# Self-attention scores from two float32r parts, with two heads in two halves of the TensorE array

## The chip, the cores and the metric

One core of one Trainium2 chip (trn2) runs the whole program. The metric is the device time of one execution in microseconds (us). The engines have these names in the rows: PE is TensorE (PEld its weight loads), DVE is VectorE, ACT is ScalarE, POOL is GpSimd, and SPq is the queue of SyncE, which issues nearly all DMAs here.

## The reference, cut to what matters

Two batches of 1024 tokens with 256 features pass through a layer of cross-attention, self-attention and a GELU network, then routed experts, a second cross-attention with a prefix, and a ternary network. The change touches the self-attention of the first layer, 16 heads of 16 features in each batch, so 32 heads of 1024 queries and 1024 keys:

```
q, k, v = split_heads(x @ sq_w + sq_b), ...(sk), ...(sv)
scores = einsum('bqhd,bkhd->bhqk', q, k) / sqrt(16)
probs  = softmax(scores, axis=-1)
out    = einsum('bhqk,bkhd->bqhd', probs, v)
```

and the ternary weights of the last network, `clip(round(w / mean|w|), -1, 1)`, which are made beside the self-attention.

## The kernel before, in words

The program has a setup, a part "a" (cross-attention, and the projections of the self-attention, for each batch in turn), a stage "b0", the loop "b" over the 32 heads, a short part "w" (the ternary weights are transposed) and a long part "c" (all the rest). In "a" and "c" the order of the steps is written out by hand (`ORDER_A`, `ORDER_C`): every engine walks the same list and does its share of each step. In "a", step QK makes queries and keys of 512 tokens: PE multiplies (`self_qk`, L929), ACT takes each result out of PSUM twice (L1267 as a bf16 piece, L1268 as float32), DVE makes a second and a third bf16 piece from the rest (`pieces`, L1511, three operations L1516 to L1518), and SP stores the pieces in DRAM (`store_pieces`, L627). Step SV makes values (DVE L1524).

Scores need more than bf16. So a head's operands QX and KX lie in 96 rows (`QROWS`): three query pieces times three, two or one key pieces. `load_head` (L639) fetches them from DRAM with six DMAs. In `KX` three more rows hold ones, and in `QX` three rows hold minus the maximum of each query, in three bf16 pieces.

For a head the work comes in this order:

- `max_scores` (PE L950): 128 queries x 1024 keys in two matmuls; DVE takes the maximum (L1545). Two pairs of PSUM banks take turns, TR and the upper half of SCR.
- `split` on POOL (L1897) splits the maxima in three bf16 pieces, `maxima_transpose` on PE (L962) turns them, `maxima_rows` on DVE (L1557) copies them to `MT`, and `move_maxima` on SP (L653) writes them as three rows into QX with three DMAs.
- `t_scores` (PE L992): 128 keys x 1024 queries over 99 rows, two matmuls into two PSUM banks; ACT takes the exponential (L1283). Each matmul waits for the exponential before the last one, which frees its bank.
- `values` (PE L1003): probabilities times values and ones, four column groups of 32; the result is copied by ACT (L1276), turned by PE (L788), divided by DVE (L1563, L1566) and stored by SP (L651).

PE's program in a head: for each of eight key tiles `t_scores(kt)`, `values(kt - 1)` (the last tile's values come after the first scores of the next head) and `max_scores` of the head two later. The loop is unrolled by four heads, and at the fourth head the values are finished before the next group begins. The last two heads have no `max_scores`. The maxima of head n + 1 are turned at kt = 2 and copied by DVE at kt = 3 of head n. Between its maxima DVE also makes the signs of the ternary weights (L1591, L1594), and POOL multiplies them by the scale (L1922).

"b0" comes before the loop: after part "a" SP waits for all stored pieces, loads heads 0 to 2, then the ternary weights and two more weights (L665 to L668). PE and DVE make the maxima of heads 0 and 1. ACT meanwhile sums the absolute ternary weights (L1296, L1298). The first rows of maxima are moved, and the loop starts with PE's L992.

Of the kernel before, what the change touches and what calls it, by code (L numbers as in the profile page):

```python
# [30 lines left out]
DH = D // H  # L31
# [22 lines left out]
QROWS = 6 * DH  # L54
NS = 2 * TB + E - 1
UNROLL = 4
# [176 lines left out]
class Signal:  # L233

    TRIPS = {"setup": 1, "a": B, "b0": 1, "b": NH // UNROLL - 1, "blast": 1, "w": 1, "c": 1}

# [76 lines left out]
def build(nc, A, out):  # L315
    ctx = ExitStack()
    with ctx:
# [22 lines left out]
        PC = shared[:, o:o + 3072].bitcast(BF16).rearrange("p (e c n) -> p e c n", e=4, c=3)  # L340
        PTB = shared[:, o:o + 2048].rearrange("p (r n) -> p r n", r=2)
        o += 3072
        KB0 = shared[:, o:o + B * CHUNK_HEADS * SC].rearrange("p (b n) -> p b n", b=B)
        QX = [shared[:, o + 512 * j:o + 512 * (j + 1)].bitcast(BF16) for j in range(UNROLL)]
        KX = [shared[:, o + 2048 + 512 * j:o + 2048 + 512 * (j + 1)].bitcast(BF16) for j in range(UNROLL)]
        assert o + 4096 <= 3 * 4096
# [53 lines left out]
        HM = sb("HM", [128, 4, N])  # L400
        pscale = sb("pscale", [128, D])
# [12 lines left out]
        GB = MW[:, 4:8, :].rearrange("p (r j) d -> p r j d", r=2)  # L414
        tri = over("tri", [128, 128], BF16, "mask0")
# [35 lines left out]
        MT = sb("MT", [24, 128], BF16)  # L451
# [28 lines left out]
        scratch = nc.dram_tensor("pieces", [2, 3, NH * DH, S], BF16)  # L480
# [14 lines left out]
        def count(group):  # L495
# [33 lines left out]
        sq_full = Signal(sem("max_scores_full"), b0=2 * QT_PER_HEAD, b=UNROLL * QT_PER_HEAD,  # L529
                         blast=(UNROLL - 2) * QT_PER_HEAD)  # L530
        sq_done = Signal(sem("maxima_ready"), **sq_full.per)
        aux_full = Signal(sem("transposes_full"), 1, b0=1, b=2 * UNROLL, blast=2 * UNROLL - 1)
        aux_done = Signal(sem("transposes_taken"), 1, **aux_full.per)
        st_full = Signal(sem("t_scores_full"), 1, b=UNROLL * 16, blast=UNROLL * 16)
        st_done = Signal(sem("t_probs_ready"), 1, **st_full.per)
        pv_full = Signal(sem("head_out_full"), 1, b=UNROLL, blast=UNROLL)
        pv_done = Signal(sem("head_out_done"), 1, **pv_full.per)
        vh_ready = Signal(sem("head_values_ready"), b0=2, b=UNROLL, blast=UNROLL - 2)
        m_split = Signal(sem("maxima_split"), b0=2, b=UNROLL, blast=UNROLL - 2)
# [6 lines left out]
        signs_ready = Signal(sem("weight_signs_ready"), b=1 + KD, blast=1 + KD)  # L546
        tern_ready = Signal(sem("ternary_ready"), b=1, blast=1)
        mask1_ready = Signal(sem("mask1_ready"), setup=1)
        setup_done = Signal(sem("setup_done"), setup=1)
        d_head = [sem(f"head_loaded_{j}") for j in range(UNROLL)]  # L550
# [11 lines left out]
        def aux_value(tl, j, last, output):  # L562

            n = 0
            for jj in range(j + 1):
                n += not (last and jj == UNROLL - 1)
                if jj < j or output:
                    n += jj >= 1
            return Tally(tl.part, tl.i).next(aux_done, n)
# [5 lines left out]
        def _(sp):  # L575
            with nc.allow_non_contiguous_dma(reason="biases and small transposed loads"):
# [41 lines left out]

                for b in range(B):  # L620
# [6 lines left out]
                    def store_pieces(k):  # L627
                        for e in range(2 * KD):
                            sp.wait_ge(pc_ready.sem, tl.next(pc_ready))
                            dst = scratch[e // 2, :, :, :].rearrange("c r s -> r c s")[  # L630
                                bass.ds(b * D + (e % 2) * 128, 128), :, k * N:(k + 1) * N]
                            sp.dma_start(dst, PC[:, e]).then_inc(d_pieces, 16)

                    tl.walk(order_a, groups, {"PN": store_x1, "QK": store_pieces})
# [4 lines left out]
                def load_head(n, j):  # L639

                    src = scratch[:, :, bass.ds(n * DH, DH), :]
                    for c, r, m in ((0, 0, 3), (1, 3, 2), (2, 5, 1)):
                        rows = slice(r * DH, (r + m) * DH)
                        sp.dma_start(QX[j][rows, :], src[0, c].unsqueeze(0).to_broadcast([m, DH, S]))\
# [1375 lines left out]
```

## Time and profile before

| what | value |
|---|---|
| median of 3 runs | 1222.73 us (1219.84 to 1222.77) |
| profiled execution, its own time | 1223.43 us |
| its span | 1221.7 us |
| granted TensorE clock, mean | 0.944 |
| busy: PE, DVE, ACT, POOL | 90%, 68%, 50%, 23% |

The span is what the profile covers; 1.7 us lie around it. PE is busy most of the time, but busy includes waits inside the pipeline, so starts of matmuls say more than their durations. A line of a timeline gives the start, the length from the first start to the last end, engine, line of the kernel, output and inputs, and how many instructions are merged. A float32 matmul appears as two instructions.

### The profile page before, as it was taken

What the parts mean: (1) busy time and instruction counts of PE and PEld (TensorE: products, weight loads), DVE (VectorE), ACT (ScalarE), POOL (GpSimd) and SP (SyncE); (2) the same over time, 40 slices, a digit from 0 to 9 for tenths busy, and PEclk for the clock granted to TensorE, in tenths of its full rate; (3) what the DMA queues carried; (4) which work ended last, traced back from release to release, by engine and by line L of the source; (5) the groups of instructions that cost most, each with busy time, mean ns of one, the idle gap of its engine ahead of it and who ended that gap; (6) DMA issues with size and microseconds to landing.
All of it is one profiled execution on the core that took longest, in us unless ns stands there. A gap on an engine that the chain in (4) does not pass through costs nothing.

```text
span 1221.7 us, 20881 instructions
## 1 busy us (share of the span) xinstructions
PE 1101.5 (90%) x7648; PEld 603.6 (49%) x7648; DVE 829.6 (68%) x1453; ACT 610.7 (50%) x1159; POOL 285.8 (23%) x651
## 2 busy tenths in 40 slices
PE   6699689858999999999999889894989999999998
PEld 3366356502333333333333445663678877667665
DVE  1568658777888888888887327645374576987665
ACT  2265256406676766767667522130223345656643
POOL 3211212000100101001001124327238554621010
PEclk7799889958999999999999988987999999999999
DMA  7302100261122121221211331001015431110000
GB/s 193 55 11 70 60 2 23 91 196 61 34 68 60 39 63 34 69 62 35 63 34 40 126 105 35 9 9 69 27 57 178 148 100 44 39 35 2 12 11 31
DMA packets 102851, 73.34 MB, mean 60 GB/s; under 512 B 50738, under 2 KB 93791, under 8 KB 102495
## 3 DMA queue, kind: packets, MB, share of 16 engines
q1 hardware_dynamic: 99679, 63.61, 17.8%
q0 software_dynamic: 3072, 8.39, 2.1%
q8 instruction: 63, 1.03, 0.4%
q14 instruction: 37, 0.30, 0.1%
HBM read 42.94 MB, written 28.84 MB: 59 GB/s over the span
## 4 chain that ended last, share of the span: by engine, by line
PE 74%; DVE 13%; ACT 4%; issue 3%; POOL 2%; DMA 2%; SPq 1%; DVEq 0%; ACTq 0%; POOLq 0%
PE OUT L782 14%; PE TR L782 14%; PE OUT L1003 12%; PE SCR L992 9%; PE TR L788 8%; PE SCR L950 5%; PE TR L950 5%; PE TR L892 2%; PE OUT L788 2%; PE SCR L876 2%; ACT PTS L1239 2%; DVE small L1430 2%; PE SCR L869 2%; DVE small L1545 1%; POOL dispatched L1977 1%
## 5 line engine op out<-in xcount | busy, mean ns | idle before, releaser
L1283 ACT ACTIVATE shared<-SCR 128x512 f32<-128x512 f32 x512 | 277.8, 594 | 113.7 <-PE SCR L992 112.7
L1545 DVE TENSOR_REDUCE small<-TR 128x1 f32<-128x1024 f32 x128 | 156.8, 1225 | 48.9 <-PE TR L950 46.4
L1545 DVE TENSOR_REDUCE small<-SCR 128x1 f32<-128x1024 f32 x128 | 156.6, 1223 | 22.0 <-PE SCR L950 18.4
L1003 PE MATMUL OUT<-shared,HM 128*32 128x256 f32 x2048 | 163.7, 391 | 0.4 <-ACT shared L1283 0.4
L992 PE MATMUL SCR<-shared 99*128 99x512 bf16 x512 | 157.0, 382 | 4.7 <-DMA shared<-MT 4.4
L1856 POOL TENSOR_SCALAR small<-small 128x1 f32<-128x1 f32 x112 | 28.2, 252 | 398.1 <-DVE small L1431 396.4
L782 PE MATMUL TR<-xT,fifo 128*128 128x512 f32 x224 | 113.1, 665 | 2.8 <-ACT xT L1219 2.8
L950 PE MATMUL TR<-shared 96*128 96x512 bf16 x256 | 81.1, 400 | 15.4 <-DMA shared<-pieces 13.6
L1901 POOL CAST small<-small 128x8 bf16<-128x8 f32 x32 | 7.4, 231 | 371.4 <-DVE small L1545 371.4
L1219 ACT ACTIVATE xT<-TR 128x256 f32<-128x256 f32 x96 | 35.6, 382 | 115.8 <-PE TR L788 115.2
L1003 PEld LDWEIGHTS OUT<-shared,HM 128*32 128x32 f32 x2048 | 40.3, 108 | 102.7 <-issue 98.8
L1239 ACT ACTIVATE PTS<-TR 96x512 f32<-96x512 f32 x128 | 70.8, 591 | 35.6 <-PE TR L788 34.5
L992 PEld LDWEIGHTS SCR<-shared 99*128 99x128 bf16 x512 | 49.7, 97 | 76.2 <-ACT shared L1283 16.1
L950 PE MATMUL SCR<-shared 96*128 96x512 bf16 x256 | 81.3, 401 | 0.6
L788 PE MATMUL TR<-identf,P 128*96 128x128 f32 x512 | 74.0, 285 | 7.6 <-ACT PTS L1239 6.0
L782 PEld LDWEIGHTS TR<-xT,fifo 128*128 128x128 f32 x224 | 47.0, 216 | 61.7 <-issue 52.7
L1474 DVE TENSOR_REDUCE small<-SCR 128x16 f32<-128x1232 f32 (+1 forms) x32 | 48.7, 1521 | 38.9 <-PE SCR L876 38.8
L1857 POOL TENSOR_TENSOR small<-small 128x1 f32<-128x1 f32 x112 | 67.5, 603 | 9.3
L788 PEld LDWEIGHTS TR<-identf,P 128*96 128x96 f32 x512 | 53.1, 129 | 26.9 <-ACT PTS L1239 15.6
L782 PE MATMUL OUT<-fifo,shared 128*128 128x256 f32 x256 | 59.4, 386 | 3.2 <-ACT shared L1326 1.6
L782 PE MATMUL TR<-xT,fcT 128*128 128x512 f32 x128 | 55.7, 593 | 0.0
L782 PEld LDWEIGHTS OUT<-fifo,shared 128*128 128x128 f32 x256 | 48.4, 193 | 12.1 <-ACT shared L1326 2.6
(236 smaller groups left out, 1816.4 us busy)
## 6 DMA issues: line engine op xcount, KB each, us to landing
pieces<-shared SPq DMA_DIRECT2D x16, 384.0 KB, 2.5
shared<-pieces SPq DMA_DIRECT2D x64, 96.0 KB
HM<-dispatched SPq DMA_DIRECT2D x46, 128.0 KB, 2.2
expert_out<-HM SPq DMA_DIRECT2D x46, 128.0 KB
dispatched<-HB SPq DMA_DIRECT2D x6, 768.0 KB, 3.7
shared<-pieces SPq DMA_DIRECT2D x64, 64.0 KB
shared<-in_L_ffn_w SPq DMA_DIRECT2D x4, 1024.0 KB, 10.7
X<-in_x SPq DMA_DIRECT2D x1, 2048.0 KB, 9.0
```

Source lines behind the costliest of these rows:

```text
L782: ins = nc.tensor.matmul(dst, l, r, start=(n == 0), stop=(n == len(pairs) - 1))
L788: ins = nc.tensor.transpose(dst[0:m, n * width:n * width + p], s, ident[0:p, 0:p])
L950: ins = nc.tensor.matmul(pair[:, hf, :], QX[j][0:QROWS, kt * 128:(kt + 1) * 128], KX[j][0:QROWS, hf * 512:(hf + 1) * 512], start=True, sto ...
L992: nc.tensor.matmul(SCR[:, bank, :], KX[j][0:QROWS + 3, kt * 128:(kt + 1) * 128], QX[j][0:QROWS + 3, hf * 512:(hf + 1) * 512], start=True, ...
L1003: ins = nc.tensor.matmul(PV[32 * g:32 * g + 32, 0:256], VH[:, j % 2, kt, :], PTB[:, kt % 2, g * 256:(g + 1) * 256], start=(kt == 0), stop= ...
L1219: nc.scalar.activation(dst[:, :, c:c + 128], bank[:, 0:256].rearrange("p (k n) -> p k n", k=KD), ACT.Copy)\
L1239: nc.scalar.activation(PTS[0:KP, 4 * g:4 * g + 4, :], bank[0:KP].rearrange("p (h n) -> p h n", h=4), ACT.Copy)\
L1283: nc.scalar.activation(PTB[:, kt % 2, hf * 512:(hf + 1) * 512], SCR[:, bank, :], ACT.Exp, scale=DH ** -0.5).then_inc(st_done.sem, 1)
L1474: chain(nc.vector.tensor_reduce(mx, v, AX, ALU.max))
L1545: nc.vector.tensor_reduce(nm[:, r, kt:kt + 1], pair.rearrange("p h n -> p (h n)"), AX, ALU.max, negate=True)\
L1856: chain(nc.gpsimd.tensor_scalar(ve[:, r:r + 1], mv[:, r, 1:2], EPS, None, ALU.add))
L1857: nc.gpsimd.tensor_tensor(rstd[:, r:r + 1], ve[:, r:r + 1], minus_half, ALU.pow)\
```

## The change

The scores are made from two float32r parts of each number in place of three bf16 pieces, so a head has 48 rows (query parts 1, 1, 2 against key parts 1, 2, 1) plus three for the maxima. Heads lie in one of two halves of the partitions: head n in rows 0 to 50 or 64 to 114, by n // 2 % 2, and each QX and KX buffer holds two heads. In the loop each `t_scores` matmul of head n is followed at once by a `max_scores` matmul of head n + 2, which lies in the other half; `values` follow. The loop is no longer unrolled by four, so nothing is drained at each fourth head. Heads 0 to 3 are loaded at the beginning of batch 1 of part "a". The rows of ones come from 12 DMAs in the setup in place of four DVE memsets. A head's load is four DMAs, of 4 KB rows. The maxima are turned at kt = 3 (PE) and copied by ACT in place of DVE, behind its exponentials of kt = 3; the first such copy stands behind ACT's sums of the ternary weights. The head's output is divided by DVE at kt = 6 in place of 5. All ternary work is on POOL: three or four operations per piece. `pieces` on DVE is one operation in place of three.

```diff
-QROWS = 6 * DH
+QROWS = 3 * DH
-UNROLL = 4
+SLOTS = 4
...
+        PC = [over(f"pieces_{e}", [128, 2, N], F32R, "shared", o + 1024 * e) for e in range(2 * KD - 1)]
+        QX, KX = ([over(f"{name}_{r}", [128, S], F32R, "shared", o + 1024 * (2 * r + c)) for r in range(2)]
+                  for c, name in enumerate(("head_q", "head_k")))
...
-        scratch = nc.dram_tensor("pieces", [2, 3, NH * DH, S], BF16)
+        scratch = nc.dram_tensor("pieces", [2, 2, NH * DH, S], F32)
...
+        def half(n):
+            return 64 * (n // 2 % 2)
...
+                def load_head(n):
+                    src = scratch[:, :, n * DH:(n + 1) * DH, :]
+                    q, k, g = QX[n % 2][:, :].bitcast(F32), KX[n % 2][:, :].bitcast(F32), half(n)
+                    sp.dma_start(q[g:g + 2 * DH, :], src[0, 0].unsqueeze(0).to_broadcast([2, DH, S])).then_inc(d_head[n % SLOTS], 16)
+                    sp.dma_start(k[g:g + 2 * DH, :], src[1]).then_inc(d_head[n % SLOTS], 16)
+                    sp.dma_start(q[g + 2 * DH:g + 3 * DH, :], src[0, 1]).then_inc(d_head[n % SLOTS], 16)
+                    sp.dma_start(k[g + 2 * DH:g + 3 * DH, :], src[1, 0]).then_inc(d_head[n % SLOTS], 16)
...
+                    if b > 0:
+                        sp.wait_ge(d_pieces, DC + 16 * 4 * BLOCKS)
+                        for n in range(SLOTS):
+                            load_head(n)
...
+            def max_scores(tl, n, kt, hf):
+                if hf == 0:
+                    tl.next(sq_full)
+                    pe.wait_ge(sq_done.sem, tl.back(sq_full, 2))
+                rows = slice(half(n), half(n) + QROWS)
+                ins = nc.tensor.matmul(SQ[kt % 2][:, hf, :], QX[n % 2][rows, kt * 128:(kt + 1) * 128],
+                                       KX[n % 2][rows, hf * 512:(hf + 1) * 512], start=True, stop=True)
...
+                for kt in range(QT_PER_HEAD):
+                    for hf in range(2):
+                        t_scores(tl, n, kt, hf)
+                        if n + 2 < NH:
+                            max_scores(tl, n + 2, kt, hf)
                     if kt > 0:
+                        values(tl, n, kt - 1, 2)
+                    elif n > 0:
+                        values(tl, n - 1, QT_PER_HEAD - 1, 2)
+                    if kt == 3 and n + 1 < NH:
+                        maxima_transpose(n + 1)
+                    if kt == 5 and n >= 1:
+                        head_out_transposes(n - 1)
...
+            def maxima_rows(n):
+                act.wait_ge(aux_full.sem, taken["max", n])
+                act.wait_ge(d_m2, n * 48)
+                nc.scalar.activation(MT[:, :], AUX.bitcast(BF16)[0:24, 0:128], ACT.Copy).then_inc(aux_done.sem, 1)
...
-                        chain(nc.vector.tensor_tensor(rest, RR[:, e % 2, :], PC[:, e, 0, :], ALU.subtract))
-                        chain(nc.vector.tensor_copy(PC[:, e, 1, :], rest))
-                        nc.vector.tensor_tensor(PC[:, e, 2, :], rest, PC[:, e, 1, :], ALU.subtract)\
+                        nc.vector.tensor_tensor(PC[e][:, 1, :], RR[:, e % 2, :], PC[e][:, 0, :].bitcast(F32), ALU.subtract)\
...
+            def ternary(tl, chain, w, m, scaled):
+                below = TN[:, 0:w.shape[-1]]
+                chain(nc.gpsimd.tensor_scalar(below, w, wscale[:, 2, m:m + 1], None, ALU.is_lt))
+                chain(nc.gpsimd.tensor_scalar(w, w, wscale[:, 1, m:m + 1], None, ALU.is_gt))
+                ins = nc.gpsimd.tensor_tensor(w, w, below, ALU.subtract)
```

## Rows read from the trace of the kernel before

**Rows 1.** Windows: stretches before b0, b0, the loop with and without maxima:
```profile
0.00:256.77 256.77, 198.74 (x1527) 126.79 (x1527) 155.55 (x304) 113.66 (x197) 48.67 (x165) 0.89 0.23 65
256.77:280.09 23.32, 16.53 (x33) 2.33 (x34) 19.54 (x21) 5.37 (x20) 2.07 (x10) 0.50 0.65 207
280.09:667.00 386.91, 383.18 (x2972) 122.99 (x2972) 320.89 (x373) 270.47 (x513) 37.62 (x154) 0.99 0.19 52
667.00:686.63 19.63, 19.00 (x162) 5.66 (x161) 2.20 (x8) 16.52 (x33) 0.93 (x5) 1.00 0.07 9
```
**Rows 2.** Timeline of one key tile, PE and ACT (start, length):
```profile
406.86 0.60 PE L950 MATMUL TR<-shared 96*128 96x512 bf16 x2
407.31 0.60 PE L992 MATMUL SCR<-shared 99*128 99x512 bf16 x2
407.72 1.08 ACT L1283 ACTIVATE shared<-SCR 128x512 f32<-128x512 f32 x2 [0.46 <-PE SCR L992]
407.83 0.64 PE L1003 MATMUL OUT<-shared,HM 128*32 128x256 f32 x8
408.40 0.60 PE L950 MATMUL SCR<-shared 96*128 96x512 bf16 x2
```
**Rows 3.** Groups of DVE in the loop (busy, mean ns, idle before):
```profile
L1545 DVE TENSOR_REDUCE small<-TR 128x1 f32<-128x1024 f32 x120 | 147.0, 1225 | 42.1 <-PE TR L950 39.6 <-POOL small L1904 2.2
L1566 DVE TENSOR_TENSOR HM<-OUT,small 128x128 f32<-128x128 f32 x29 | 8.4, 291 | 1.0
L1563 DVE RECIPROCAL small<-OUT 128x8 f32<-128x8 f32 x29 | 5.8, 200 | 1.0 <-DVE xT L1594 0.4
```
**Rows 4.** Timeline of the last two heads, PE and ACT:
```profile
674.27 0.61 PE L992 MATMUL SCR<-shared 99*128 99x512 bf16 x2
...
679.18 0.69 PE L992 MATMUL SCR<-shared 99*128 99x512 bf16 x2
...
682.33 2.19 ACT L1283 ACTIVATE shared<-SCR 128x512 f32<-128x512 f32 x4 [0.44 <-PE SCR L992]
...
686.63 0.38 ACT L1276 ACTIVATE OSB<-OUT 128x256 f32<-128x256 f32 x1 [0.76 <-PE OUT L1003]
```
**Rows 5.** Line L992: weight loads (min, median, max ns):
```profile
L992 PEld LDWEIGHTS SCR<-shared x512: 95/97/152, 280.1 to 684.6; 99*128 99x128 bf16 x171
```
**Rows 6.** Timeline of a stage with float32r operands, weight load and matmul:
```profile
1210.26 0.28 PE L782 MATMUL OUT<-projT,hidH 128*128 128x256 f32 x1
1210.38 0.28 PE L782 MATMUL OUT<-projT,hidL 128*128 128x256 f32 x1
1210.26 0.19 PEld L782 LDWEIGHTS OUT<-projT,hidL 128*128 128x128 f32 x1
```
**Rows 7.** Timeline of matmuls in four row groups, and what follows:
```profile
1001.22 0.87 PE L876 MATMUL SCR<-KBW,QT 32*128 32x174 f32 x16
1002.02 0.48 PE L782 MATMUL OUT<-shared,MW 128*128 x1
```
**Rows 8.** Timeline from the last QK step to the loop:
```profile
234.33 7.13 PE L782 MATMUL TR<-xT,fifo 128*128 128x512 f32 x16 [0.47 <-ACT xT L1219]
244.70 0.69 DVE L1518 TENSOR_TENSOR shared<-HM,shared 128x512 bf16<-128x512 f32 x1
245.43 0.88 DVE L1524 TENSOR_TENSOR shared<-OUT,rows_a 128x256 f32<-128x256 f32 x2
256.77 1.01 PE L950 MATMUL TR<-shared 96*128 96x512 bf16 x2 [13.57 <-DMA shared<-pieces]
259.86 4.08 SPq L666 DMA_DIRECT2D xT<-in_L_ffn_w_proj  x1
273.94 0.42 ACT L1296 ACTIVATE XN<-xT 128x256 f32<-128x256 f32 x1 [31.01 <-DMA xT<-in_L_ffn_w_proj]
276.93 2.08 SPq L658 DMA_DIRECT2D shared<-MT  x3
279.12 0.18 ACT L1298 ACTIVATION_READ_ACCUMULATOR PTS<-xT 128x1 f32 x1
280.09 1.04 PE L992 MATMUL SCR<-shared 99*128 99x512 bf16 x2 [4.36 <-DMA shared<-MT]
```
**Rows 9.** DMAs by issue: KB each, us to landing:
```profile
pieces<-shared SPq DMA_DIRECT2D x16, 384.0 KB, 2.5
```
**Rows 10.** POOL's scaling of a ternary piece, group in the loop:
```profile
L1922 POOL TENSOR_TENSOR xT<-xT,small 128x256 f32<-128x256 f32 x7 | 4.3, 614 | 0.0
```

More of the change, by code:

```diff
@@ L559, in row @@
             return ap.rearrange("(o n) -> o n", o=1).to_broadcast([parts, ap.shape[0]])
[L562 to L569, printed above, removed]
+        taken = {("max", 0): aux_done.base["b0"] + 1}
+        for n in range(NH):
+            if n + 1 < NH:
+                taken["max", n + 1] = aux_done.base["b0"] + len(taken) + 1
+            if n >= 1:
+                taken["out", n - 1] = aux_done.base["b0"] + len(taken) + 1
+        taken["out", NH - 1] = aux_done.base["b0"] + len(taken) + 1
+        assert taken["out", NH - 1] == aux_done.total
+        def half(n):
+            return 64 * (n // 2 % 2)
         block = ctx.enter_context(nc.Block())
@@ L683, in head @@
                         sp.dma_start(xs_dram[i % B].rearrange("(s p) d -> p s d", p=128)[:, lo:hi, :], zeros).then_inc(d_zero, 16)
[L684 to L695 removed]
+                store_output(NH - 1)
                 for r in range(2):
@@ new lines, in t_scores, with values @@
+            def t_scores(tl, n, kt, hf):
+                bank = tl.slot(st_full, 2)
+                tl.next(st_full)
+                pe.wait_ge(st_done.sem, tl.back(st_full, 2))
+                rows = slice(half(n), half(n) + QROWS + 3)
+                nc.tensor.matmul(SCR[:, bank, :], KX[n % 2][rows, kt * 128:(kt + 1) * 128],
+                                 QX[n % 2][rows, hf * 512:(hf + 1) * 512], start=True, stop=True)\
+                    .then_inc(st_full.sem, 1)
+            def values(tl, n, kt, ahead):
+                pe.wait_ge(st_done.sem, tl.back(st_full, ahead))
+                if kt == 0:
+                    pe.wait_ge(pv_done.sem, tl.value(pv_full))
+                    pe.wait_ge(vh_ready.sem, n + 1)
+                for g in range(4):
+                    ins = nc.tensor.matmul(PV[32 * g:32 * g + 32, 0:256], VH[:, n % 2, kt, :],
+                                           PTB[:, kt % 2, g * 256:(g + 1) * 256], start=(kt == 0),
+                                           stop=(kt == QT_PER_HEAD - 1))
+                if kt == QT_PER_HEAD - 1:
+                    ins.then_inc(pv_full.sem, 1)
+                    tl.next(pv_full)
```

367 lines of the change are left out of this document (122 added, 245 removed).

## The prediction

> **What bounds the kernel now.** I read the windows first. The loop over heads takes 386.9 us with maxima and 19.6 us for the two heads without [rows 1], 406.5 us from its first PE start to the last head's copy [rows 8, 4], a third of the time. PE is busy 99% of it at full clock (0.99, the 2.4 GHz level), DVE 83%, ACT 70%. The timeline of one key tile shows the order in which PE spends it [rows 2]: two maxima products start at 406.86, two score products at 407.31, the values at 407.83, the next maxima at 408.40. That is 0.45 + 0.52 + 0.57 = 1.54 us per tile, and eight tiles with some 0.3 us of transposes make 12.6 us a head; 32 heads give 403 us, near the 406.5. ACT sits idle 0.46 us in each tile and waits for L992, and DVE waits for L950 (42 us for half of its maxima, [rows 3]). So PE's sequence is the bound, and whatever it sheds counts until another loop closes.
>
> Ahead of the loop lie two waits on other things. After the last pieces (DVE, until 245.4) PE stands 13.57 us, until a head's load has landed at 256.77 [rows 8]. Then b0 runs at DVE's pace, at clock 0.50 (the 1.2 GHz level) [rows 1], and the loop's first product waits until 280.09 for the rows of maxima.
>
> **The change, part by part, against the profiled execution's 1223.4 us (0.7 above the median of the runs).**
>
> *Products in two halves.* Three terms: the cost of a float32r product, whether two of them run at once, and what then closes the loop. A stage with float32r operands starts a 256-column matmul every 0.12 us [rows 6], just over 256 columns at 2.4 GHz, so a 512-column one should take some 0.22 us, what the bf16 ones take now (two in 0.45). I take a pair of a score and a maxima product at 0.22 + 0.03 us. PE's need per tile falls from 1.54 to 0.50 + 0.09 + 0.57 = 1.16 us (0.09 is what L992 now takes over its two streams before the values begin).
>
> What closes the loop then? The last two heads show it, since they have no maxima: from 674.27 to 679.18 are four tiles, 1.23 us each [rows 4], and the two heads together take 19.6 us, 1.22 a tile [rows 1], though PE would need 1.1. There each second score product waits for the exponential that frees its bank, and the values and the next tile stand behind it. This chain remains. It grows by the weight load that such a wait exposes: 0.19 us for float32r against 0.10 for bf16 [rows 6, 5], so +0.09, and by the 0.03 of the maxima products between. I get 1.22 + 0.09 + 0.03 = 1.34 us per tile, 10.7 us a head. DVE alone needs eight maxima at about 1.19 (a duration of 1.225 with ends overlapped) and 0.55 us for the head's output with its waits [rows 3], 10.0 us. ACT needs 16 x 0.53 (four in 2.19 us, [rows 4]) + 0.39 + 0.2 for the maxima's copy, 9.1 us. Both fit below 10.7, but DVE closely: it is next in line. Bounds: 10.0 us (DVE alone) to 12.6 (no overlap, as now).
>
> Loop: 30 heads x 10.7 + 2 x 10.5 (9.8 now, plus 8 x 0.09) + 0.9 for start and end = 343 us, against 406.5: **-63.5 us**. The drain at each fourth head goes with it, and the ternary signs leave DVE; they lay beside PE's work and are worth nothing by themselves. POOL takes them: at most four operations of about 0.61 us [rows 10] in a head of 10.7 us, ahead of a split that waits for the head's last maxima anyway. If that cover went, the maxima's split would be late; it has more than three tiles of slack. On SP a head's load is four issues in place of six, so what stands behind it (the maxima's rows, the output's store) is not later than now.
>
> *Pieces and the end of part a.* The last QK step is paced by PE (7.13 us for its 16 instructions, until 241.5), but DVE's three operations, 1.92 us per product, end at 245.4 [rows 8]. With one operation of 0.69 the end is 241.5 + 1.3 (ACT) + 0.7 = 243.5, 1.9 us earlier. I give the last QK of batch 0 the same 1.9, and the two QKs in the middle of a batch 0.5 each, where other work hides DVE: **-2.9 us** ahead of the last step. Bounds 0 to -6.
>
> *Early head loads.* PE no longer waits for the load; it starts b0 when the last values are out of PSUM, at 243.5 + 0.9 = 244.4 in place of 256.8. But b0 does not end by DVE alone. The first rows of maxima now stand on ACT behind its sums, which wait for the ternary weights. Those are issued when the last pieces are stored, 243.5 + 2.5 [rows 9] = 246.1 in place of 259.4, so 13.3 us earlier. Sums started at 273.94 and ended at 279.3; they will start at 260.6 and end at 266.0. Copy 0.2 and the move as now (280.09 - 276.93 = 3.16) give 269.5. DVE's 16 maxima, 244.4 + 1.1 + 19 = 264.6, are earlier. So the loop starts 280.1 - 269.5 = **10.6 us** sooner; the ends are -16 (DVE decides) and -5 (the loads land later behind the larger stores). The 12 DMAs for the rows of ones and the 16 for heads 0 to 3 lie on SP beside work of the setup and of batch 1, where only stores of tokens stand behind them. Nothing waits for those within several us.
>
> Sum: 1223.4 - 63.5 - 2.9 - 10.6 = **1146 us**. Part w and part c (535 us) stay.
>
> A rule against this change: the Trainium skill (TensorE: Matmul & The Clock Gate, Part 3, "The mechanism") says that a weight load overlaps running matmuls only when its row group differs. Its consequence is a rival below.
>
> **The rivals.**
>
> *Late rows of maxima.* The rows are turned at kt = 3 now, after three tiles and a block, near 5.1 us into a head; ACT copies at about 5.9; SP's three issues and the landing take 3.16 [rows 8], so they are there at 9.1 of 10.7 us. The slack is 1.6 us, where it was about 3. For it: four heads' worth of 4 KB rows may stand before them on the rings. If the landing grew by 3 us, each head waits 1.4 to 1.5 us: 31 x 1.45 = 45 us, time 1191. Chance 0.13.
>
> *Exposed weight loads.* The second score product and the second maxima product use the row groups of the first ones. If their loads wait until the first stream is through, 0.19 us [rows 6] come on per tile, 1.5 a head: 32 x 1.52 = 49, time 1195. Against: float32r loads start every 0.12 us though each lasts 0.19, between matmuls of the same rows [rows 6]. This is what the page's rule would do here, and the row speaks against the rule. Chance 0.13.
>
> *Halves in sequence, loads hidden.* 4 x 0.216 + 0.09 + 0.57 = 1.53 per tile, 12.65 a head: 30 x 12.65 + 22 = 401, time 1223.4 - 5.1 - 13.5 = 1205. Against it stands L876. Chance 0.07.
>
> *Slower.* The halves run in sequence and each load is exposed too: 4 x (0.216 + 0.19) + 0.66 = 2.29 us per tile on PE, 18.7 a head, 583 us for the loop, time 1386. It ends slower than before once a tile costs over 1.61 us: (406.5 + 13.5 - 22) / 30 = 13.3 us a head, less 0.4 for transposes, over 8. For it: no row shows float32r in row groups. Against: each half of it is absent where it could show [rows 6, 7]. Chance 0.06, and I add 0.01 for a clock that falls to 1.2 GHz in the loop. The heads without maxima kept 1.00 with PE streaming about 70% of the tile [rows 1, 4].
>
> *It brings nothing, some wait of its own eating all.* Chance 0.02.
>
> **How the numbers follow.** The forecast has 0.58 and its own range is 1130 to 1168: 10.3 to 11.2 us a head (-12 to +16), and the front's ends (-8 to +6). I predict 1146. The range reaches to the two rivals of 0.13 each: 1130 to 1197, with about 0.8 in it. About 0.3% is what a measurement of this kernel can tell from no change. Faster: 0.58 + 0.13 + 0.13 + 0.07 = 0.91; same 0.02; slower 0.07.
>
> **What would show it.** Right: L950 and L992 starts within 0.05 us of each other, a head every 10.7 us, DVE idle under 1 us a head, PE's first L992 near 267. L992 waiting for ACT in nearly every tile, with a weight load of 0.19 ahead of it, confirms the chain. Late maxima would show as L992 waiting for the DMA from MT at each head. Exposed loads would show as a gap of 0.4 us between first and second score products that no exponential explains. In sequence: a score and a maxima product start 0.22 us apart. Part a should end 3 to 5 us earlier. The prediction is wrong if heads take over 12 us or under 10 us, or if the loop starts after 272.

## The result and the profile after

The changed kernel takes 1173.1 us (median of 4 runs, 1169.1 to 1174.8) against 1222.8 us before (median of 4): a ratio of 0.959, 95% interval 0.954 to 0.963. The profiled execution takes 1171.8 us, its span 1169.7. The forecast was 1146 us, range 1130 to 1197.

The windows of the changed kernel, with the columns of [rows 1] (busy time of PE, weight loads, DVE, ACT, POOL with counts in brackets, then granted clock, DMA share, GB/s), b0 first and then the loop:
```profile
242.48:265.95 23.47, 17.66 (x35) 7.50 (x35) 19.89 (x21) 5.66 (x21) 3.28 (x13) 0.57 0.56 200
266.00:286.00 20.00, 19.77 (x109) 6.79 (x109) 11.02 (x9) 10.77 (x21) 3.61 (x9) 0.50 0.00 1
...
290.00:295.00 5.00, 5.00 (x37) 1.70 (x35) 3.14 (x3) 3.37 (x7) 0.00 (x0) 0.66 0.09 34
295.00:300.00 5.00, 5.00 (x46) 2.00 (x48) 4.61 (x6) 3.98 (x9) 1.07 (x6) 1.00 0.56 168
300.00:560.00 260.00, 259.56 (x2322) 103.98 (x2320) 238.51 (x234) 212.11 (x423) 64.08 (x176) 1.00 0.23 59
```
DVE is now busy 92% of the stretch from 300 to 560 (238.5 of 260), where it had 83%, so the loop is denser, as meant. But the loop runs its first 27 us at clock 0.50, the 1.2 GHz level. (It was 1.00 when b0 began and fell to 0.50 inside b0, near 245.6.) In the kernel before, it rose at 284, 4 us after the loop's start:
```profile
280.09:284.00 3.91, 3.91 (x12) 1.25 (x16) 1.88 (x2) 1.79 (x4) 0.00 (x0) 0.50 0.21 61
284.00:288.00 4.00, 4.00 (x37) 1.23 (x29) 2.41 (x5) 2.67 (x6) 0.00 (x0) 1.00 0.10 38
```

The timeline from the last QK step to the loop, to be held against [rows 8]. L784 is the product, L1494 DVE's one operation on the pieces, L952 the maxima product, L963 the score product, L1266 ACT's sums, L1259 its copy of the maxima, L673 their move:
```profile
232.22 7.13 PE L784 MATMUL TR<-xT,fifo 128*128 128x512 f32 x16 [0.47 <-ACT xT L1196]
240.76 0.69 DVE L1494 TENSOR_TENSOR pieces<-RR,pieces 128x512 fp32r<-128x512 f32 x1 [1.02 <-ACT RR L1245]
242.48 0.70 PE L952 MATMUL TR<-head_k,head_q 48*128 48x512 f32 x2 [1.39 <-issue]
244.65 0.58 SPq L679 DMA_DIRECT2D xT<-in_L_ffn_w_proj  x1
252.44 0.42 ACT L1266 ACTIVATE XN<-xT 128x256 f32<-128x256 f32 x1 [11.78 <-DMA xT<-in_L_ffn_w_proj]
262.36 0.27 ACT L1259 ACTIVATE MT<-OUT 24x128 fp32r<-24x128 bf16 x1 [4.52 <-PE OUT L984]
262.65 2.07 SPq L673 DMA_DIRECT2D head_q<-MT  x3
265.95 0.76 PE L963 MATMUL SCR<-head_q,head_k 51*128 51x512 f32 x1 [3.62 <-issue]
```
PE's 13.6 us of waiting is 1.4, and the loop starts at 265.95 instead of 280.09. POOL had split the maxima of head 0 by 254.3, but their transpose (L984) stands in PE's order behind the maxima products of head 1, so it starts only at 262.04, 7.7 us later. No run moves it.

Two key tiles of the loop, PE alone (start, length, the idle time in brackets; a matmul's row includes the load that stands exposed ahead of it):
```profile
400.46 0.49 PE L963 MATMUL SCR<-head_q,head_k 51*128 51x512 f32 x1
400.46 0.49 PE L952 MATMUL TR<-head_k,head_q 48*128 48x512 f32 x1
400.79 0.41 PE L963 MATMUL SCR<-head_q,head_k 51*128 51x512 f32 x1
400.80 0.41 PE L952 MATMUL TR<-head_k,head_q 48*128 48x512 f32 x1
401.14 0.64 PE L974 MATMUL OUT<-shared,HM 128*32 128x256 f32 x8
401.71 0.50 PE L963 MATMUL SCR<-head_q,head_k 51*128 51x512 f32 x1
401.71 0.50 PE L952 MATMUL SCR<-head_k,head_q 48*128 48x512 f32 x1
402.12 0.18 PEld L963 LDWEIGHTS SCR<-head_q,head_k 51*128 51x128 f32 x1 [0.23 <-ACT shared L1279]
402.13 0.50 PE L963 MATMUL SCR<-head_q,head_k 51*128 51x512 f32 x1
402.56 0.64 PE L974 MATMUL OUT<-shared,HM 128*32 128x256 f32 x8
```
A score and a maxima product start within 0.01 us of each other, in both pairs of both tiles. The first tile takes 1.25 us, the second 1.45: there the second pair waits for ACT's exponential, and its load of 0.18 us stands in the open. Such tiles alternate, 1.345 us on average. The largest idle times of the weight loader ahead of the score products, from 300 to 560 (us in total, times, longest):
```profile
PEld SCR L963 <- ACT shared L1279: 81.5, 257, 0.4
PEld SCR L963 <- DMA head_q<-MT: 4.0, 8, 0.6
```
The 81.5 us aren't all loss: some of these times are 0.41 us, ahead of a tile's first load while the values still stream, and the others 0.23, as at 402.12. PE itself is busy 259.6 of the 260 us.

The last two head outputs are copied here; the one before them is copied at 610.48:
```profile
621.55 0.39 ACT L1253 ACTIVATE OSB<-OUT 128x256 f32<-128x256 f32 x1
632.02 0.38 ACT L1253 ACTIVATE OSB<-OUT 128x256 f32<-128x256 f32 x1 [0.76 <-PE OUT L974]
```

Of the 51.6 us between the two profiled executions, the loop's earlier start gives 14.1 (13.5 forecast) and the loop itself 40.4 (366.1 us against 406.5, from its first score product to the last output copy; 63.5 forecast). Parts w and c take 2.6 us more (537.7 against 535.1). The 23 us missing in the loop are what the experiments had to find.

My first reading gave them to two places: some 10 us to the low clock (the first head's output comes 19.0 us after the loop's start and the second 14.3 later, where most later ones come every 11.09), and 12 us to a head of 11.1 us instead of 10.7.

### The profile page after: what moved, and what is told of

It is laid out like the page before. It is cut to its first block, busy times and chain, and to the rows that moved or that the text cites. A ratio compares the mean times of both kernels' runs of the same rounds, so it can differ in the third digit from the quotient of the medians.

```text
span 1169.7 us, 20774 instructions
## 1 busy us (share of the span) xinstructions
PE 1067.8 (91%) x7648; PEld 625.3 (53%) x7648; DVE 792.1 (68%) x1337; ACT 615.2 (53%) x1191; POOL 331.6 (28%) x724
## 4 chain that ended last, share of the span: by engine, by line
PE 75%; DVE 11%; ACT 4%; issue 3%; POOL 3%; DMA 2%; SPq 1%; DVEq 0%; ACTq 0%; POOLq 0%
PE SCR L963 16%; PE TR L784 16%; PE OUT L784 14%; PE OUT L974 12%; PE TR L790 8%; PE TR L894 2%; PE OUT L790 2%; PE SCR L878 2%; ACT PTS L1216 2%; DVE small L1409 2%; PE SCR L871 1%; POOL dispatched L1899 1%; POOL small L1784 1%; DVE small L1517 1%; PE SCR L952 1%
## 5 line engine op out<-in xcount | busy, mean ns | idle before, releaser
L963 PE MATMUL SCR<-head_q,head_k 51*128 51x512 f32 x512 | 218.2, 484 | 4.3 <-issue 3.6
L974 PE MATMUL OUT<-shared,HM 128*32 128x256 f32 x2048 | 168.8, 402 | 0.2 <-ACT shared L1279 0.2
L963 PEld LDWEIGHTS SCR<-head_q,head_k 51*128 51x128 f32 x512 | 92.9, 189 | 137.1 <-ACT shared L1279 114.8
L952 PE MATMUL SCR<-head_k,head_q 48*128 48x512 f32 x256 | 122.3, 516 | 1.2 <-DVE small L1517 0.8
L784 PE MATMUL TR<-xT,fifo 128*128 128x512 f32 x224 | 113.1, 665 | 2.8 <-ACT xT L1196 2.8
L952 PE MATMUL TR<-head_k,head_q 48*128 48x512 f32 x256 | 100.3, 474 | 2.3 <-issue 1.4
L784 PEld LDWEIGHTS TR<-xT,fifo 128*128 128x128 f32 x224 | 46.9, 215 | 61.8 <-issue 52.8
L784 PE MATMUL OUT<-fifo,shared 128*128 128x256 f32 x256 | 59.3, 386 | 3.2 <-ACT shared L1305 1.6
L784 PE MATMUL TR<-xT,fcT 128*128 128x512 f32 x128 | 55.7, 593 | 0.0
L784 PEld LDWEIGHTS OUT<-fifo,shared 128*128 128x128 f32 x256 | 48.4, 193 | 12.1 <-ACT shared L1305 2.6
## 6 DMA issues: line engine op xcount, KB each, us to landing
shared<-in_L_ffn_w SPq DMA_DIRECT2D x4, 1024.0 KB, 10.7
```

The costliest lines, as they stand in the source:

```text
L784: ins = nc.tensor.matmul(dst, l, r, start=(n == 0), stop=(n == len(pairs) - 1))
L952: ins = nc.tensor.matmul(SQ[kt % 2][:, hf, :], QX[n % 2][rows, kt * 128:(kt + 1) * 128], KX[n % 2][rows, hf * 512:(hf + 1) * 512], start=T ...
L963: nc.tensor.matmul(SCR[:, bank, :], KX[n % 2][rows, kt * 128:(kt + 1) * 128], QX[n % 2][rows, hf * 512:(hf + 1) * 512], start=True, stop=T ...
L974: ins = nc.tensor.matmul(PV[32 * g:32 * g + 32, 0:256], VH[:, n % 2, kt, :], PTB[:, kt % 2, g * 256:(g + 1) * 256], start=(kt == 0), stop= ...
```

## The experiments

**1. The two products apart.** Only the order on PE changes: both score products, the values, then both maxima products.
```diff
                         t_scores(tl, n, kt, hf)
-                        if n + 2 < NH:
-                            max_scores(tl, n + 2, kt, hf)
...
                     if kt == 5 and n >= 1:
                         head_out_transposes(n - 1)
+                    if n + 2 < NH:
+                        for hf in range(2):
+                            max_scores(tl, n + 2, kt, hf)
```

> The changed kernel with one edit: in each key tile both score products, then the values, then both maxima products (the order of the kernel before), so no score product has a maxima product of the other half beside it; operands, rows and loads stay. If the two halves really run at once in the changed kernel, this takes it away: a head goes from 11.1 us to 12.6 to 12.9 us (two streams of 0.43 us and 0.09 us of switch come on per tile, less what the chain of exponentials leaves idle), time near 1220. Rival, that the halves bring nothing and the gain is only the lost drain at each fourth head and the early loads: a head stays at 11.1 us, time 1172. The clock at the start of the loop: if it stayed low because TensorE had gaps in its stream there, it rises within about 5 us of the loop's start here, as in the kernel before; if it stayed low because a product in half the rows counts for less, it stays at 1.2 GHz for over 20 us here too.

Measured: 1196.6 us (one run), a head every 12.24 us, the loop 395.6 us. That is less than the 12.6 to 12.9 us and 1220 us that I expected, but far from the rival's 11.1. Standing beside each other is worth 1.13 us a head, and 29.5 of the 40.4 us that the loop gained. Without it the loop is still 10.9 us shorter than before; the lost drain, the operands and DVE's lighter work changed together there, and no run splits them. The clock was at 0.50 here too, until about 283, 19 us after the loop's start:
```profile
266.00:282.00 16.00, 16.00 (x87) 5.79 (x87) 8.43 (x7) 8.22 (x16) 1.25 (x2) 0.50 0.00 1
282.00:284.00 2.00, 2.00 (x16) 0.65 (x12) 1.23 (x1) 1.40 (x3) 0.14 (x1) 0.65 0.00 0
```
PE was busy for all of those 16 us. So idle time that the profile would show isn't what kept the clock down.

**2. Products in all rows ahead of the loop.** Twelve matmuls of 512 columns over all 128 rows, whose result nobody reads, stand behind the first maxima transpose, where PE would wait for the rows of maxima.
```diff
             maxima_transpose(0)
+            for _ in range(12):
+                nc.tensor.matmul(OUT[:, 1, :].rearrange("p (a n) -> p a n", n=128), identb[:, :],
+                                 onesb[:, :].unsqueeze(1).to_broadcast([128, 4, 128]), start=True, stop=True)
```

> The changed kernel with 12 dense bf16 matmuls of 512 columns, on no one's data, put on TensorE behind the first transpose of maxima, where it waits 3.9 us for the rows of maxima. Theory: the loop lost about 10 us because TensorE's clock stayed at 1.2 GHz for its first 27 us; the dense work lifts the clock before the loop and the loop holds it, so the first two heads take 12.5 + 11.1 us in place of 19.0 + 14.3, less up to 1.3 us for matmuls that run past the wait: 1163 to 1166. Rival: the loop's start is slow for another reason (first loads, POOL's ternary work, DVE), or the clock falls again at once: 1172 to 1174.

Measured: 1156.8 us (median of 5 runs, 1156.0 to 1162.4), ratio 0.947, interval 0.944 to 0.950. Windows:
```profile
264.00:268.00 4.00, 3.96 (x12) 1.31 (x10) 0.00 (x0) 0.23 (x1) 3.50 (x7) 0.57 0.01 2
268.00:272.00 4.00, 3.58 (x29) 1.43 (x29) 3.67 (x3) 3.36 (x7) 0.38 (x1) 1.00 0.00 0
```
The clock is at 1.00 from 268 and stays there. The loop takes 355.9 us in place of 366.1, and every head 11.10 us, the second one too. So the low clock cost 10.2 us inside the loop. The spans differ by 9.4 us (1160.3 and 1169.7), as the loop starts 1.15 us later in this execution; the medians differ by 16.3, and the profiles explain only the 9.4. The profiled execution is the slowest of the five (1162.4 us; the others take 1156.0 to 1157.1). The median lies below my 1163 to 1166; the heads came as the theory said.

**3. The same twelve in 48 rows.** The number and the columns are as above, the rows as in b0.
```diff
-                nc.tensor.matmul(..., identb[:, :],
-                                 onesb[:, :].unsqueeze(1).to_broadcast([128, 4, 128]), start=True, stop=True)
+                nc.tensor.matmul(..., identb[0:48, :],
+                                 onesb[0:48, :].unsqueeze(1).to_broadcast([48, 4, 128]), start=True, stop=True)
```

> As the version with 12 products of 512 columns ahead of the loop, but they use 48 rows of the array instead of 128. If the granted clock follows how dense the stream is, the result is that of the full-row products: first output copy about 12.4 us after the loop's start, 1155 to 1160 us. If it follows how many rows are at work too, the clock stays at half speed as in the changed kernel: first output copy 18 to 19 us after the start, second head above 13 us, 1170 to 1176 us.

Measured: 1164.4 us (one run). The clock did not rise with them:
```profile
264.00:268.00 4.00, 3.74 (x13) 1.96 (x11) 0.87 (x1) 1.08 (x2) 3.07 (x4) 0.50 0.00 0
...
284.00:288.00 4.00, 4.00 (x32) 1.15 (x24) 2.72 (x3) 2.56 (x6) 0.30 (x1) 0.66 0.15 36
```
The first output copy comes 19.2 us after the loop's start, as the second theory has it. The second head (11.9 us) is faster than expected, as the clock rose near 286.7 and not near 293, and the time lies below that theory's 1170 to 1176 us. So with the same number of products and columns the clock was up at the loop's start with 128 rows, and was not with 48.

**4. The type, and two halves at once.** Experiment 6 below runs the loop's products in bf16, in the same rows, and there the clock rose 7.6 us into the loop. So the type could have been the cause as well as the rows. Two more kernels with twelve products tell these apart: one with float32r operands over 128 rows (and 112 columns of weights), one with twelve pairs of bf16 products in rows 0 to 47 and 64 to 111.
```diff
-                nc.tensor.matmul(..., identb[:, :],
-                                 onesb[:, :].unsqueeze(1).to_broadcast([128, 4, 128]), start=True, stop=True)
+                nc.tensor.matmul(..., onesr[:, :],
+                                 onesr[:, 0:64].unsqueeze(1).to_broadcast([128, 8, 64]), start=True, stop=True)
```

> Again twelve products of 512 columns ahead of the loop, over 128 rows, but with float32r operands (and 112 columns of weights). Open is whether the rows alone decide, or the type too, since with bf16 products in half the rows the clock rose 7 us into the loop and with float32r ones after 18 to 27. If rows decide, the clock is at full speed when the loop begins, as with the twelve in bf16: first output copy about 12.4 us after the loop's start. If float32r streams don't lift it, the copy comes 18 to 19 us after the start.

Measured: 1157.2 us (one run), first output copy 12.2 us after the loop's start, the loop 355.9 us.
```profile
264.00:266.00 2.00, 2.00 (x10) 1.06 (x8) 0.00 (x0) 0.08 (x1) 1.82 (x3) 0.87 0.00 0
```
```diff
+                for g in (0, 64):
+                    nc.tensor.matmul(..., identb[g:g + 48, :],
+                                     onesb[g:g + 48, :].unsqueeze(1).to_broadcast([48, 4, 128]), start=True, stop=True)
```

> Twelve pairs of bf16 products of 512 columns ahead of the loop, one in rows 0 to 47 and one in rows 64 to 111, at once. If what counts is how many rows are at work at a time, 96 of them lift the clock as 128 did: first output copy 12.4 to 13.5 us after the loop's start. If products in a half don't count, also two at a time, it stays low: copy 18 to 19 us after the start.

Measured: 1161.8 us (one run), first output copy 12.6 us after the start, the loop 355.9 us.
```profile
264.00:266.00 2.00, 2.00 (x12) 0.96 (x10) 0.00 (x0) 0.00 (x0) 1.82 (x3) 0.50 0.00 0
266.00:268.00 2.00, 1.55 (x10) 0.55 (x7) 1.20 (x1) 1.47 (x3) 1.17 (x2) 0.95 0.00 0
```
So the clock rose with float32r as with bf16, and with 96 rows in two halves as with 128. From the first of the twelve, it rose after 5.5 us in bf16 over 128 rows (near 267.4), after 3.9 in float32r over 128 rows (near 264.5) and after 5.5 in pairs (near 266.2), in one profiled execution each: these times don't order the kinds. What the four streams say together is that the outcome went with the rows at work at a time and not with the type. One doubt stays: the twelve pairs are also 24 products in the same time, and no stream here has that many in 48 rows alone. A question stays as well, since the loop's own pairs hold 99 rows and the clock stayed low under them for 27 us. They differ from the dense pairs in what stands between them: waits for ACT, and weight loads, 0.28 to 0.34 us each at this clock. The bf16 loop, where a load takes 0.10, rose sooner. That fits, but no kernel here changed the gaps alone, so the moment at which the clock rises in the loop by itself (7.6 us after its start in bf16, 19 to 27 in float32r) stays open.

**5. A third bank for the score products.** The second tile's wait is for a bank. Here the bank for transposes joins the two for scores in a ring of three, through which the scores, the next head's maxima and the turned output pass in PE's order; ACT copies the turned output to SBUF, and DVE divides from there.
```diff
+        ST = [SCR[:, 0, :], SCR[:, 1, :], AUX]
...
-                bank = tl.slot(st_full, 2)
-                pe.wait_ge(st_done.sem, tl.back(st_full, 2))
+                pe.wait_ge(st_done.sem, m - 3)
...
+                nc.scalar.activation(TOKM[:, n % 2, :], ST[item["out", n] % 3][:, 0:256], ACT.Copy)
```

> The changed kernel with three PSUM banks in turn for the score products in place of two. The third is the bank of the transposes; these now take turns in the same ring, and ACT copies the head's turned output to SBUF, from where DVE divides it. Theory: the steady 11.1 us of a head is the chain exponential, bank free, weight load, score product, values; with a third bank no score product waits for the exponential before the last, and DVE decides: 10.1 to 10.4 us a head, 30 heads save 21 to 30 us, time 1143 to 1152. Rival: TensorE's own work (with the switches between its row and column groups) decides; then a head stays within 0.3 us of 11.1, time 1165 to 1173.

Measured: 1156.7 us (median of 4 runs, 1148.4 to 1158.1), ratio 0.945, interval 0.941 to 0.949. A head takes 10.73 us on average, the loop 351.7 us with its first 20 us still at 0.50. So the chain through two banks is worth 0.37 us a head. Neither theory holds as it stands: the head is above the 10.1 to 10.4 us of the one and just outside the 0.3 us of the other, and the time lies between their ranges. The waits of this kernel misled me:
```profile
PEld SCR L973 <- DMA head_q<-MT: 15.2, 24, 1.1
```
I took this line (24 times, once a head) for late rows of maxima as the next bound.

**6. The products in bf16.** Score and maxima products read only the upper 16 bits of each value; the lower bits of both parts are left out of the computation.
```diff
+                q, k = (v[n % 2][:, :].bitcast(BF16).rearrange("p (n two) -> p n two", two=2)[:, :, 1] for v in (QX, KX))
```

> The changed kernel with score and maxima products over the upper 16 bits of each number, read in place as bf16 with a step of two; so the lower bits of the parts are left out of the products. Rows, halves and waits stay; the weight load of a product takes about 0.10 us in place of 0.18. Theory: each tile exposes one such load, so a head falls from 11.1 us by 8 x 0.09 = 0.7 us to 10.4, time 1150. If two loads are exposed per tile it falls by 1.3 us, down to DVE's 10.1 to 10.3. Rival: the loads lie beside other work; 11.1 us stay, time 1172.

Measured: 1140.2 us (one run), a head every 10.58 us, the loop 341.1 us; the loads take 0.09 us instead of 0.18, and the clock rose near 272. The group of the score products:
```profile
L965 PE MATMUL SCR<-head_q,head_k 51*128 51x512 bf16 x393 | 141.6, 395 | 8.3 <-DMA head_q<-MT 5.6
```
The exposed loads are part of the head: it is 0.52 us shorter, with 0.09 less for each load; I had expected 0.7. That is some 16 of the 25.0 us that the loop is shorter. Most of the rest lies in the first two heads, whose second copy comes 8.9 us sooner, as the clock rose 7.6 us after the loop's start and not 27. I hadn't put that into the 1150, and parts w and c were 5.2 us shorter in this execution. Here PE truly stood idle for the rows of maxima (5.6 us in the stretch), and without that the head would be near 10.35.

**7. Both additions together, the ring and the twelve products.**

> The ring of three banks and the 12 full-row products ahead of the loop, together. If the cold clock and the output's transposes are two separate losses, their gains add: the ring alone gave 1156.7 us, the 12 products take the 10 us of cold clock and cost about 1.6 us themselves, but a faster first stretch is again held to the pace of the ring, so 1143 to 1149 us, the head near 10.7 us, the first head below 11.5 us. Rival (late rows of maxima already bind from the first head, so that a warm clock there buys only part): 1150 to 1156 us.

Measured: 1144.6 us (median of 5 runs, 1140.6 to 1145.5), ratio 0.936, interval 0.934 to 0.938: 12 us on top of either. The gains add: in the loop 24.3 us, against 14.4 for the ring and 10.2 for the products alone. In the medians they give 28.5 of 32.8 us. A head takes 10.68 us: half of them 10.5 to 10.6, but four of 31 take 11.1 to 11.25. One such head in the chain of waits:
```profile
378.78 0.66 SPq L679
...
379.48 4.10 DMA head_q<-MT
...
383.62 0.49 PE SCR L973
```
PE stood idle 0.53 us there for the rows of maxima.

**8. The maxima's rows one key tile earlier.** The previous kernel, with the transpose, its copy and its move behind key tile 2.
```diff
-                    if kt == 3 and n + 1 < NH:
+                    if kt == 2 and n + 1 < NH:
```

> As the ring with the 12 full-row products, but the next head's maxima are transposed, copied and sent off one key tile earlier (behind key tile 2 instead of 3, about 1.3 us). If the late rows are what makes each head of the ring version wait about 0.6 us ahead of its first product, the wait is gone or small, and DVE's eight reductions with the output's division set the head: 10.1 to 10.4 us, 1133 to 1142 us. Rival (the maxima themselves come late, since DVE's split and GpSimd's steps end only behind key tile 2, so the transpose then waits in PE's order and holds up the products behind it): the head stays at 10.7 us or grows, 1146 to 1156 us.

Measured: 1144.6 us (median of 5 runs, 1143.8 to 1145.3), a head every 10.64 us. The median doesn't move, the head by 0.04 us, and my theory falls. The windows and the waits of this kernel say why:
```profile
300.00:560.00 260.00, 257.82 (x2425) 98.88 (x2425) 246.65 (x245) 229.12 (x465) 66.33 (x183) 1.00 0.24 64
```
```profile
PEld SCR L973 <- DMA head_q<-MT: 12.5, 24, 0.7
```
The wait is still there 24 times, though the rows now start 1.2 us earlier. Most of it is no stall: the loader is idle 0.41 us ahead of the first load of every tile, while the values stream, and 24 x 0.41 = 9.8 of the 12.5 us (and of the 15.2 of experiment 5) is that gap, put down to whatever semaphore came last. The 2.7 us left are 0.11 us a head, about what the mean of 10.64 has over the 10.52 of the undelayed heads. They remain because the rows, sent earlier, landed more slowly: in the 12 heads where the chain of waits goes through this DMA it takes 4.4 to 5.0 us, against 3.6 to 4.2 in experiment 7. PE itself is busy 257.8 of 260 us. What is left is PE's order of work:
```profile
398.65 0.49 PE L973 MATMUL SCR<-head_q,head_k 51*128 51x512 f32 x1
398.76 0.19 PEld L973 LDWEIGHTS OUT<-head_q,head_k 51*128 51x128 f32 x1
398.99 0.39 PE L973 MATMUL OUT<-head_q,head_k 51*128 51x512 f32 x1
399.88 0.50 PE L973 MATMUL SCR<-head_q,head_k 51*128 51x512 f32 x1
401.11 0.20 PEld L796 LDWEIGHTS OUT<-identf,OSB 128*128 128x128 f32 x2 [0.41 <-issue]
401.48 0.50 PE L973 MATMUL SCR<-head_q,head_k 51*128 51x512 f32 x1
```
A tile takes 1.23 us (398.65 to 399.88), and the output's two transposes 0.37 (401.11 to 401.48). Eight tiles, the transposes and some 0.2 us at the maxima's turn give 10.4, near the 10.52 of the undelayed heads. DVE, whose duration of 1.23 us also fills a tile, is at 95%, so by the tile alone it could be the bound as well. The last two copies of the output tell:
```profile
586.12 0.39 ACT L1267 ACTIVATE OSB<-OUT 128x256 f32<-128x256 f32 x1
596.63 0.39 ACT L1267 ACTIVATE OSB<-OUT 128x256 f32<-128x256 f32 x1
```
Between them no maxima are made, DVE works for 0.5 us only, and the head takes 10.51 us too.

**9. The output's transposes apart.** The kernel of experiment 2, with one transpose behind key tile 4, one behind 6, and the division behind 7.
```diff
-                    if kt == 5 and n >= 1:
-                        head_out_transposes(n - 1)
+                    if kt in (4, 6) and n >= 1:
+                        head_out_transposes(n - 1, ((kt - 4) // 2,))
```

> The version with 12 full-row products ahead of the loop (1156.8 us, head 11.10 us), with the output's two transposes set apart, one behind key tile 4 and one behind key tile 6, and the division behind key tile 7. If the 0.33 us that the transposes add to the chain comes from standing together where the chain between PE and ACT has no room, each single one (0.2 us) partly fits into PE's waits on ACT (0.41 us ahead of each weight load, 0.23 of it beyond the load itself): head 10.8 to 10.95 us, 1147 to 1152 us. Rival (PE's order is the chain, so what is put into it is paid wherever it stands): head 11.05 to 11.2 us, 1155 to 1160 us.

Measured: 1163.1 us (median of 4 runs, 1161.6 to 1164.0), a head every 11.25 us; most take 11.2, some 11.6 to 11.9. Each transpose takes its own time of PE's order:
```profile
407.16 0.33 PE L790 MATMUL OUT<-identf,OSB 128*128 128x128 f32 x1
407.42 0.50 PE L963 MATMUL SCR<-head_q,head_k 51*128 51x512 f32 x1
```
It is 0.26 us from the transpose to the next score product, and the same at the second (410.10 to 410.36): 0.52 in all against 0.37 together, and the 0.15 between them is what the head grew. The rival held, with a head slightly above its 11.05 to 11.2.

**10. The head loads late again.** The changed kernel, with the loads of heads 0 to 3 behind all of part a's stores; the pairs stay.
```diff
                     if b > 0:
                         sp.wait_ge(d_pieces, DC + 16 * 4 * BLOCKS)
-                        for n in range(SLOTS):
-                            load_head(n)
...
                 for r in range(2):
                     sp.wait_ge(d_x1[r], DC + 16 * T // 2)
+                for n in range(SLOTS):
+                    load_head(n)
```

> The changed kernel with the loads of heads 0 to 3 put back behind part a's last stores and loads, the pairs kept. If the early loads are what brought the loop's start from 280.1 to 266.0 us, it goes back to 276 to 280 us and the whole to 1183 to 1187 us. Rival (the earlier start comes from part a or the ones' load, not from the early loads): the start stays below 270 us and the time below 1176 us.

Measured: 1188.0 us (one run). The loop starts at 287.02, later than I expected and later than before the change. From the timeline:
```profile
254.01 1.19 PE L950 MATMUL TR<-head_k,head_q 48*128 48x512 f32 x2 [13.22 <-DMA head_k<-pieces]
257.76 10.38 SPq L677 DMA_DIRECT2D xT<-in_L_ffn_w_proj  x1
278.19 0.42 ACT L1264 ACTIVATE XN<-xT 128x256 f32<-128x256 f32 x1 [37.81 <-DMA xT<-in_L_ffn_w_proj]
283.47 0.25 ACT L1257 ACTIVATE MT<-OUT 24x128 fp32r<-24x128 bf16 x1
```
The early loads do two things. PE's b0 starts 11.5 us earlier (242.48 against 254.01), and the ternary weights' load isn't behind 16 loads of heads: it lands 7.8 us after its issue in the changed kernel, and 20.4 us after it here, where the issue itself takes 10.4. ACT's sums wait for it and hold the maxima's copy until 283.5. The early loads are worth 21.1 us of the loop's start. The spans differ by 16.2 us; the loop took 1.7 and parts w and c 3.2 us less in this execution.

## Why the prediction was right, and where its sum was off

The time fell in the range and the mechanism was the forecast one; one term of the sum, the loop's 343 us, was too small by 23.

*Two at once, loads hidden.* Right. The pairs start within 0.01 us. The last heads, which have no maxima products, take 11.07 and 10.47 us here, so at 11.09 a head with them pays next to nothing for them. Experiment 1 shows what it would pay: 1.13 us. The rivals in sequence and with exposed loads fell: in experiment 8 the second pair's load (398.76) lies under the first pair's stream in the same rows, and the second pair takes 0.23 us (399.15 to 399.38 in the chain of waits). The Trainium skill (TensorE: Matmul & The Clock Gate, Part 3, "The mechanism") has in its list a load overlap only where the row group differs; the paragraph ahead of the list also allows it for a load into a background weight buffer, and no row here shows which buffer a load takes. By the list alone, I estimate, every tile would have 0.18 us more. The rows disagree with that, and the measurement decides.

*What closes the loop.* Right in kind: the score product that waits for the exponential, a load of 0.18 us ahead of it. The third bank took the wait away and the tile fell to 1.23. That the tile came out at 1.345 us against my 1.34 is in part luck: I had added 0.09 for the load and 0.03 for the maxima products, but in the last heads, which have none, the tiles take 1.34 as well (622.71 to 625.39 for two).

*The head.* Here the sum failed, by 0.4 us a head and 12 us in all. I took 9.8 us for a head without maxima, from the window of 19.6 us [rows 1], and read it as eight tiles of 1.22 with nothing left over. But that window doesn't hold two whole heads: it begins 0.26 us after an output copy, and its last head has the scores of only seven tiles in it, as no next head follows. By the output copies of the kernel before, its first head without maxima takes 10.12 us (666.74 to 676.86) and only the last one 9.77 (676.86 to 686.63, [rows 4]). In the 10.12 are the output's two transposes, which the tiles of 1.23 that I had picked don't show: they stand on the same chain and cost about 0.35 us. With the right base, 10.12 + 8 x 0.12 = 11.08, against 11.10 measured. The 0.12 is what the tile rose by, and not my split of it: for the first head without maxima 10.12 + 8 x 0.09 gives 10.84, and 11.07 was measured. So 0.03 us a tile have no cause that a run shows. Experiment 9 shows that the transposes cost time wherever they stand.

*The clock.* Not foreseen at all; 10.2 us. I had a rival for a clock that falls inside the loop at full density, and none for one that stays low at its start. [Rows 1] showed b0 at 0.50, and the loop's mean of 0.99 hid when it rose. Before, it did so 4 us into the loop, with products in 96 to 99 rows; now each product of b0 and each score product is in 48 or 51 rows of a half. In experiments 2 to 4 the clock was up at or just after the loop's start behind streams in 128 or 96 rows at a time, and was not behind one in 48. Why it stays low for 27 us under the loop's own pairs is open. The remaining 1 us of the 23 is in the loop's first head.

*The front.* The sum was right (14.1 us against 13.5), but not by its own path. The last QK step ended 3.9 us earlier (240.76 against 244.70) against 4.8, largely since it began 2.1 earlier instead of 2.9. The weights landed 7.8 us after their issue and not 14.1, so ACT's sums were done at 257.8, and the 16 maxima, at DVE's pace, set the transpose at 262.0 and with it the start. I had named that as an end of the range. What went wrong is that I carried a duration over from a queue that had just been filled with 18 loads; experiment 10 shows it at 20.4 behind 16 others.

*Late rows of maxima.* In the changed kernel hardly: 4.0 us over 24 heads, and by experiment 8 most of that is the loader's ordinary gap. PE itself stood idle for them for 0.3 us in all. Once the head fell to 10.5 us, single heads did show it.

*DVE next in line.* Wrong. With the bank wait gone, PE's own order closed the loop again, at 99% busy with DVE at 95%, and a head without maxima took no less (experiment 8).

*Part c.* Its 2.6 us are no effect that I can show. The eleven kernels of the experiments have the same code there, and it took 532.5 to 538.7 us in their profiled executions; before it was 535.1.

## What to carry to other kernels

When a forecast takes a chain's period from a stage without the removed work, measure it between two equal events of consecutive rounds (the same copy, head by head), not as a window divided by a count: rare steps that hide between picked tiles are in the one and fall out of the other.
